# Clearing the sorted edge rows: blind from tile 1000 on, elsewhere only the padding, with the tile tables built inside the scatter

## What is computed

```python
h = relu(layernorm(x))
x = x + L0(h, edge_attr_64, ...)      # per edge: leaky_relu([h[dst], edge_attr] @ w1 + b1) @ w2 + b2, summed by src
x = x + L1(relu(layernorm(x)), ...)   # graph attention with 100 relation weights
x = x + L2(relu(layernorm(x)), ...)   # GCN: normalised sum over neighbours, mish
x = x + L3(relu(layernorm(x)), ...)   # mean over neighbours, relu
```

## Time and profile before

| | us |
|---|---|
| median of three runs | 3377.89 |
| the profiled execution, and its span | 3380.8, 3379.1 |
| block 1 | 0 to 180.8 |
| block 2: until the first indirect transfer | 181 to 280.2 |
| block 2: indirect transfers | 280.2 to 1310.5 |
| block 3 and the layers behind | 1318 to 3379.1 |

### The profile page before, as it was taken

One profiled execution on the slowest core, in us unless ns is written; L12 is line 12 of the kernel. 1 busy time (PEld: TensorE's weight loads), 2 busy tenths in 40 slices (PEclk: granted clock), 3 DMA queues, 4 the chain that ended last, 5 costly groups with the idle time before them and its releaser, 6 DMA issues. The chain is left out here.

```text
span 3379.1 us, 87741 instructions
## 1 busy us (share of the span) xinstructions
PE 2511.1 (74%) x20390; PEld 1974.6 (58%) x20391; DVE 2597.0 (77%) x8325; ACT 1489.4 (44%) x3942; POOL 1952.3 (58%) x2344
## 2 busy tenths in 40 slices
PE   1433555555555554999999999999999239989899
PEld 1322334333334343999999999999997214445455
DVE  7863777777777773999999999999997779983501
ACT  2011222222222222677777777777775655452200
POOL 1005777777777777899999999999996000000000
PEclk9975677677777776999999999999999559999999
DMA  9993222222222223888888888888886669869766
GB/s 381 414 414 129 78 78 83 78 78 78 77 79 78 78 68 104 236 240 234 242 239 235 240 239 234 242 238 236 241 239 226 255 282 343 301 219 315 249 220 208
DMA packets 738172, 696.84 MB, mean 206 GB/s; under 512 B 48524, under 2 KB 637275, under 8 KB 734779
## 3 DMA queue, kind: packets, MB, share of 16 engines
q1 hardware_dynamic: 516770, 536.77, 47.6%
q10 hardware_dynamic: 195544, 104.71, 12.7%
q0 software_dynamic: 25792, 54.52, 4.9%
HBM read 340.91 MB, written 354.90 MB: 206 GB/s over the span
## 5 line engine op out<-in xcount | busy, mean ns | idle before, releaser
L855 POOL DMA_INDIRECT sorted_rows<-rows,posi x806 | 785.1, 974 | 338.7 <-issue 221.4
L1147 DVE SCALAR_TENSOR_TENSOR acc<-acc,keep,pm 128x256 f32<-128x256 f32 x1504 | 715.7, 476 | 70.9 <-issue 23.9
L965 POOL TENSOR_SCALAR ohs_e<-iota,rt 128x128 f32<-128x128 f32 x1128 | 666.2, 607 | 12.4 <-DMA rt<-sorted_rows 12.4
L803 PE MATMUL s_peq<-sb_w1bb,eT 128*128 128x256 f32 x806 | 352.5, 531 | 398.9 <-ACT eT L658 379.9
L1074 PE MATMUL pm<-ohw_e,ohs_e 128*128 128x128 f32 x3008 | 609.1, 283 | 0.0
L974 POOL TENSOR_TENSOR hid<-pre_e,excess 128x512 f32<-128x512 f32 x376 | 482.8, 1284 | 117.2 <-ACT excess L1001 117.2
L1080 PE MATMUL px<-PN,dT 128*128 x4512 | 498.1, 219 | 0.4 <-ACT dT L1014 0.4
L1020 ACT ACTIVATE ohw_e<-ohd_e,rt 128x128 f32<-128x128 bf16 x1504 | 490.5, 397 | 0.0
L1074 PEld LDWEIGHTS pm<-ohw_e,ohs_e 128*128 128x128 f32 x3008 | 461.8, 194 | 0.0
L803 PEld LDWEIGHTS s_peq<-sb_w1bb,eT 128*128 128x128 f32 x806 | 172.8, 265 | 441.1 <-ACT eT L658 432.7
L1091 PE MATMUL ps<-hid,ohs_e 128*128 128x129 f32 x3008 | 424.3, 283 | 0.5 <-POOL hid L974 0.5
(11 more groups left out here) (317 smaller groups left out, 4206.3 us busy)
## 6 DMA issues: line engine op xcount, KB each, us to landing
count_matrices<-acc SPq DMA_DIRECT2D x1504, 128.0 KB, 2.6
sorted_rows<-zrow SPq DMA_DIRECT2D x188, 528.0 KB, 10.5
rt<-sorted_rows ACTq DMA_DIRECT2D x184, 528.0 KB, 4.6
gab<-count_matrices SPq DMA_DIRECT2D x60, 1280.0 KB, 6.0
arb<-count_matrices SPq DMA_DIRECT2D x25, 1664.0 KB, 8.8
ab<-count_matrices SPq DMA_DIRECT2D x25, 1600.0 KB, 9.3
arb<-count_matrices SPq DMA_DIRECT2D x25, 1536.0 KB, 8.5
ef<-in_edge_attr_dram SPq DMA_DIRECT2D x58, 364.0 KB
```

The source lines that it names most:

```text
L803: nc.tensor.matmul(pe_q[:, q % 2, 0:2 * D], eT[:, q % 2, :], w1bb[:], start=True, stop=True).then_inc(s_q, 1)
L855: pool.indirect_dma_start(sortd, bass.IndirectOffsetOnAxis(ap=posi[:, h, c:c + 1], axis=0), rows[:, h, c, :], None).then_inc(s_sc[h], 16)
L965: last = nc.gpsimd.tensor_scalar(ohs[:, k % BUFS, j, :], iota128[:], rt[:, k, j, D + 1:D + 2], None, ALU.is_equal)
L1147: nc.vector.scalar_tensor_tensor(acc[:, k % SUMS, j, :], before, keep[:, at:at + 1] if isinstance(at, int) else keep[:, ds(at, 1)], pm[:, ...
```

## The change

- **Clearing.** SP clears only tiles 1000 to 1503 blindly: 63 transfers of 8 tiles, all in block 1. Of tiles below 1000 only padding is cleared, rounded up to a multiple of 16 rows: for each bin the last 64, the 64 before them, the 32 or the 16 rows in front, as the bits of its padding say. The indices are computed on DVE, stored to device memory, loaded back with five bins in each of 125 partitions, and used by 20 indirect transfers on POOL (four sizes, five columns each; a row of such a transfer has 33,792, 16,896 or 8,448 bytes). Two more clear the tiles that round up a source tile's last bin to groups of four, and four more the free tiles below 1000. An index beyond tile 1000 writes nothing. POOL issues these 26 at the end of block 1.
- **One-hots** are made 52 columns at a time, with 16-bit inputs and outputs that are all contiguous along the columns.
- **Order of block 1.** All one-hots come first; the layer norm, the scans, and the counts' arithmetic follow; the transposes of H stand apart from the counting, and the projections of the nodes come last. ACT takes over half of the copies of PN and HT and all of the small weights.
- **Tile tables.** The 36 + 12 passes move into block 2, between places (0,1) and begin (1,0) on DVE; no transposes are needed, since the table's layout is another. They are stored by ACT before the last chunk and loaded within it.
- Several buffers share memory (`tmem`, `S`, `H`, `keep`), and POOL clears 26 columns instead of two whole buffers at the start of block 2.

The diff, cut to its core:

```diff
-                CLEARED = TT // ZR * 7 // 10
+PADS = ((192, 64, 1), (128, 64, 2), (32, 32, 0), (16, 16, 0))
+EDGE = 1000
+            BLIND = EDGE // ZR
...
 block 1, SP:
                     sp.wait_ge(s_z, 2)
-                    with sp.Fori(0, CLEARED) as n:
-                        sp.dma_start(zv[ds(n, 1)].squeeze(0), zrow[:].rearrange("p k w -> p (k w)")).then_inc(s_zd, 16)
+                    with sp.Fori(BLIND, TT // ZR) as n:
+                        sp.dma_start(zv[ds(n, 1)].squeeze(0), zrow[:, 0:ZR, :].rearrange("p k w -> p (k w)")).then_inc(s_zd, 16)
...
 block 1, ACT:
                     act.wait_ge(s_dv, 3)
-                    act.dma_start(rowinc.rearrange("(a b) -> a b", a=NT), cnt[:, 6, :]).then_inc(s_bo, 16)
-                    act.wait_ge(s_bo, 16)
+                    act.dma_start(rowinc.rearrange("(a b) -> a b", a=NT), cnt[:, 6, :]).then_inc(s_st, 16)
+                    act.wait_ge(s_dv, 4)
+                    act.dma_start(padr.rearrange("k (s d) -> s k d", s=NT), pout[:]).then_inc(s_st, 16)
+                    act.dma_start(fullr, fout[:]).then_inc(s_st, 16)
+                    act.wait_ge(s_st, 48)
+                    with nc.allow_non_contiguous_dma(reason="five bins in each partition"):
+                        act.dma_start(padi[:], padr.rearrange("k (p c) -> p k c", p=PADP)).then_inc(s_pi, 16)
+                        act.dma_start(fulli[:], fullr.rearrange("s (j c) -> (s j) c", c=2)).then_inc(s_pi, 16)
                     act.dma_start(incb[:], rowinc.partition_broadcast(P)).then_inc(s_bo, 16)
...
 block 1, POOL:
+                    def clear(index, parts, size):
+                        spots = sortd.rearrange("(n s) w -> n (s w)", s=size)
+                        pool.indirect_dma_start(
+                            spots, bass.IndirectOffsetOnAxis(ap=index, axis=0),
+                            zrow[0:parts, 0:size, :].rearrange("p k w -> p (k w)"), None,
+                            bounds_check=EDGE * P // size - 1, oob_is_err=False).then_inc(s_cl, 16)
+                    pool.wait_ge(s_z, 6)
+                    pool.wait_ge(s_pi, 32)
+                    for k, (bits, size, back_) in enumerate(PADS):
+                        for c in range(BINS // PADP):
+                            clear(padi[:, k, c:c + 1], PADP, size)
+                    for c in range(2):
+                        clear(fulli[:, c:c + 1], 3 * NT, P // 2)
+                    pool.wait_ge(s_dv, 5)
+                    for c in range(4):
+                        clear(freei[:, c:c + 1], FREE, P // 2)
...
 block 1, DVE (one-hots):
-                        nc.vector.tensor_tensor(ohs[:, n % 2, 0:w, :], iota32[:].unsqueeze(1).to_broadcast([P, w, QP]),
-                                                tile[:, 1, c].unsqueeze(2).to_broadcast([P, w, QP]), ALU.is_equal)
+                        nc.vector.tensor_tensor(ohs[:, n % 2, :, 0:w], rep32[:, :, 0:w],
+                                                tile[:, 1, c].unsqueeze(1).to_broadcast([P, QP, w]), ALU.is_equal)
...
 block 2, SP:
-                    with sp.Fori(CLEARED, TT // ZR) as n:
-                        sp.dma_start(zv[ds(n, 1)].squeeze(0), zrow[:].rearrange("p k w -> p (k w)")).then_inc(s_zd, 16)
 block 2, DVE:
                     positions(0, 0, True)
                     places(0, 1)
+                    tables()
                     begin(1, 0, False)
                     positions(0, 1, True)
 block 2, ACT, around the last chunk:
+                    act.wait_ge(s_ts, 1)
+                    act.dma_start(tilef.rearrange("(p j) -> p j", j=TCOL), tilk[:]).then_inc(s_to, 16)
+                    act.dma_start(tiler.rearrange("k (p j) -> p k j", j=TCOL), tili[:, 0:3, :]).then_inc(s_to, 16)
                     step(BODIES - 1, False, True)
+                    act.wait_ge(s_to, 32)
...
+                    act.dma_start(keep[:], tilef[0:TT].partition_broadcast(P)).then_inc(s_tl, 16)
 block 2, POOL:
-                    nc.gpsimd.memset(ef[:], 0.0).then_inc(s_pad, 1)
-                    nc.gpsimd.memset(rows[:], 0.0).then_inc(s_pad, 1)
-                    pool.wait_ge(s_zd, 16 * (TT // ZR))
+                    nc.gpsimd.memset(rows[:, :, :, D + 3:D + 4], 0.0).then_inc(s_pad, 1)
+                    pool.wait_ge(s_zd, 16 * (TT // ZR - BLIND))
+                    pool.wait_ge(s_cl, 16 * (len(PADS) * (BINS // PADP) + 6))
```

More of the change, by code:

```diff
@@ L113, in build @@
         brow = {}
-        for name in ("b1", "bs", "bn"):
+        for name in ("bs", "bn"):
             brow[name] = tsb("row_" + name, [1, D])
@@ L276, in _ @@
-                    act.wait_ge(s_to, 32)
+                        if t % 4 == 3 and t >= 7:
+                            turned(t // 4 - 1)
+                    for g in range(NT // 4 - 1, NQ):
+                        turned(g)
+                    act.wait_ge(s_dv, 3)
+                    act.dma_start(rowinc.rearrange("(a b) -> a b", a=NT), cnt[:, 6, :]).then_inc(s_st, 16)
+                    act.wait_ge(s_dv, 4)
+                    act.dma_start(padr.rearrange("k (s d) -> s k d", s=NT), pout[:]).then_inc(s_st, 16)
@@ new lines, in _ @@
+                    for g in range(NQ + 1):
+                        if g < NQ:
+                            first(g)
+                        if g >= 1:
+                            second(g - 1)
+                    act.wait_ge(s_w, 1)
+                    for k, name in enumerate(("WsT", "WnT")):
+                        nc.scalar.activation(wl[name][:], px[:, 1, (2 + k) * P:(3 + k) * P], ACT.Copy)
+                    nc.scalar.activation(wturn[:].rearrange("p a b -> p (a b)"), px[:, 1, 0:2 * P], ACT.Copy).then_inc(s_wc, 1)
@@ L301, in _ @@
                     line(iota128[:], [[1, P]])
-                    nc.gpsimd.memset(later[:], 1.0).then_inc(s_pc, 1)
-                    pool.wait_ge(s_pc, 2)
+                    for k, (bits, size, back_) in enumerate(PADS):
+                        nc.gpsimd.memset(pmask[:, k:k + 1], bits)
+                        if not back_:
+                            nc.gpsimd.memset(pmask[:, k + 2:k + 3], -size)
+                    nc.gpsimd.memset(later[:], 1.0).then_inc(s_z, 1)
+                    pool.wait_ge(s_z, 4)
@@ new lines, in _ @@
+                    link(last)
+                    for k, (bits, size, back_) in enumerate(PADS):
+                        if not back_:
+                            last = nc.vector.scalar_tensor_tensor(pidx[:, 0, k, :], cnt[:, 0, :], float(P // 2 // size), part[:, k - 2, :],
+                                                                  ALU.mult, ALU.subtract)
+                    link(last)
+                    nc.vector.tensor_tensor(pout[:], pidx[:, 0, :, :], pidx[:, 1, :, :], ALU.add)
@@ L455, in _, with turn @@
+                    nc.vector.tensor_copy(lo[:], raw[:, 0:2, :])
+                    nc.vector.tensor_copy(typ[:], raw[:, 2, :])
+                    for g in range(NQ + 1):
+                        if g < NQ:
+                            rest(g)
+                        if g >= 1:
+                            third(g - 1)
+                    nc.vector.tensor_tensor(X[:], X[:], c2bc[:].unsqueeze(1).to_broadcast([P, NT, D]), ALU.add)
                 @block.tensor
                 def _(pe):
+                    def turn(g):
+                        if g >= 2:
+                            pe.wait_ge(s_ln["copied"], g - 1)
+                        pe.wait_ge(s_ln["h"], min(4 * g + 4, NT))
+                        for t in range(4 * g, min(4 * g + 4, NT)):
+                            last = nc.tensor.transpose(tp[:, g % 2, (t % 4) * P:(t % 4 + 1) * P], H[:, t, :], ident[:])
+                        last.then_inc(s_ln["turned"], 1)
@@ L463, in project @@
                             nc.tensor.matmul(px[:, g % 2, o:o + D], HT[:, t * P:(t + 1) * P], wl["w1a"][:], start=True, stop=False)
-                            last = nc.tensor.matmul(px[:, g % 2, o:o + D], ones[0:1, :], brow["b1"][:], start=False, stop=True)
+                            last = nc.tensor.matmul(px[:, g % 2, o:o + D], ones[0:1, :], b1bc[0:1, :], start=False, stop=True)
                         last.then_inc(s_pn, 1)
-                    pe.wait_ge(s_con, 3)
+                    pe.wait_ge(s_con, 1)
                     for n in range(NS):
```

387 lines of the change are left out of this document (222 added, 165 removed).

## The result

The changed kernel takes 3476.6 us (median of four runs, 3462.4 to 3482.2) against 3376.7 for the kernel before in the same session: a ratio of 1.0289, 95% interval 1.0256 to 1.0322. It is **slower by 100 us**, where 85 us of gain were forecast. The profiled execution took 3482.2 us, its span is 3480.4.

A forecast was written before the change was run, and what follows sets the result against it. Clearing was taken to hold the scatter's start, POOL's calls to pace the rest. Block 2 at 138 plus 73.5 us to second positions puts call 14 at 211.5, 85 us earlier: 3380.8 becomes 3295, median 3293; range 3278 to 3330.

The forecast's parts named there:

- Where the change is decided: Start of POOL's scatter call 14: moves from 296.9 to 211.5, 85 us earlier; later calls and blocks go on as they are.
- Clears and counts: Block 1: SP's 63 clears issued until 89 us, one-hot counting done at 53, POOL's clearing calls starting at 104.
- rival 2: One-hot compares in block 1 stay at the old speed: counting ends 24 us later, call 14 at 236, 3317 us; chance 0.07.
- The price of a call: POOL's 26 indirect clearing calls in block 1 take 1.28 us each, until 137.
- rival 3: POOL's clearing calls cost by their bytes: POOL leaves block 1 at 294, call 14 at 368, 3448 us; chance 0.07.
- Landing: Padding's 26.7 MB land in 65 us at 414 GB/s, 83 with 12.4 of 16 engines; landed at 189 us.
- Rival 1: Padding lands late: five engines a call, 95 us, call 14 at 218, 3299 us; one engine, 126 us, 3330; chance 0.2.
- Start of block 2: POOL, PE with ACT, and DVE finish block 1 at 134 to 137, so block 2 starts at 138 instead of 181.
- The tables: DVE's tables in block 2 take 33.2 us, second positions ready 73.5 us in; padding's landing covers all but 5 us.
- Rival 4: No gain: the scatter's start is not bound by clearing and call 14 stays; chance 0.02.

The follow-up runs named there:

- e3: The changed kernel with 128 index rows instead of 125 in the twenty padding calls, the three added out of range: 3362.2 us, 0.994 to 0.997 of the kernel before.
- e1: The changed kernel with the 26 indirect clearing calls moved from the end of POOL's block 1 to the head of its block 2: 3437.7 us.
- e12: e8 with the ten calls of 32 and 16 rows and the four free ones moved to the head of POOL's block 2: 3310.3 us.
- e8: The changed kernel with 128 index rows in all 26 calls, bins dealt one by one to partitions, tables at the end of DVE's block 1: 3315.0 us.
- e2: The changed kernel with the tile tables computed at the end of DVE's block 1 instead of inside the scatter: 3434.2 us.
- e5: The changed kernel with 128 index rows in the twenty padding calls and the tile tables at the end of DVE's block 1: 3330.6 us.

## Why the prediction was wrong, step by step

- **Where the change is decided: right.** Call 14 moved by 103.1 us, the span by 101.3; the pace behind it is unchanged (1.276 us a call), and so is what follows: 2069.9 us from call 806 to the end, 2069.6 before.
- **Clears and counts: nearly right.** The 63 clears were issued by 90.7 (89 forecast). Compares of 1664 elements took 1.02 us (1.0), so rival 2 falls:

```profile
21.80 1.02 DVE L420 TENSOR_TENSOR S<-keep,tile 128x1664 f16<-128x1664 f16 x1
...
36.10 1.03 DVE L420 TENSOR_TENSOR S<-keep,tile 128x1664 f16<-128x1664 f16 x1 [6.46 <-PE hist L572]
```

  The counting still ended at 61 instead of 53: the fifth step began at 36.1 (33 forecast), and three later waits of DVE for PE, 5.6 us in all, were not in the sum. POOL's first call came at 109.4 (104 forecast, although 91 and two times 5 make 101).
- **The price of a call: 1.28 forecast, 1.49 measured** at 125 rows and 1.27 at 128. It does not go by bytes, so rival 3, the only one that made the kernel slower, falls: the time did rise, but by another road. The 26 calls took 40 us instead of 33, under the landing.
- **Landing: the first step that failed.** "At 414 GB/s ... 65 us", at most 83, "because nothing suggests that the load is spread anew". Measured 218 us. The step took a rate from direct transfers of 128 partitions and corrected it only for idle engines, in blocks of eight partitions that no row shows. What the runs showed in its place: an indirect call's landing goes by how its rows are cut (102 us with 128 rows, same bytes, e3). Rival 1 named the right cut, a call of 125 rows on five engines, and its sign, a first scatter call behind 200, came (351.5). But it priced the call by the bytes of the busiest engine at full speed: 95 us. The busy engines ran at half that speed (175 GB/s at 0.84), and the load was more uneven than it reckoned: over the last 78 us the share was a quarter or less on average.
- **Start of block 2: the second.** "POOL leaves block 1 at 137 ... All three agree, so block 2 starts at 138". This took a transfer to be over for its engine once issued. For SP that holds. SP's queue in the kernel before, its last clears of block 1 (start, time until the last was issued):

```profile
159.16 21.19 SPq L232 DMA_DIRECT2D sorted_rows<-zrow  x16
```

  They were issued until 180.35, block 2 began at 181.0, and a clear takes 10.5 us to land, so block 2 did not wait for the last of them to land. For POOL's indirect transfers it does not hold (e1, and e12 against e8): the block's end waited for all of them.
- **The tables: right in size, wrong in cover.** 73.5 us from the start of block 2 to call 14 were forecast, 72.3 measured. The cover was to be the landing; but since the barrier stands behind the landing, none of it was left, and the 32 us came on top (e2).
- **Rival 4 falls too:** clearing held the start of the scatter as before, only for longer.

Together: block 2 at 327.7 instead of 138 is 190 us. With the landing as forecast (83 + 2 us from 109.4) block 2 would have begun near 194, since it waits for that: some 56 us of the 190 are the barrier and a first call 5 us late, some 133 the landing. Without the barrier the same landing would have cost less, since call 14 of e1 is 27 us earlier although its calls start 34 us later. With 128 rows (e3) the change is a gain of 0.5%, with the tables ahead of the barrier as well (e5) of 1.4%.

## What to carry to other kernels

A transfer's price is its shape: the same 26.7 MB landed in 84 to 329 us, depending on how many index rows a call had and on which partitions they stood (the 329 include POOL's stops at 127 rows); here it paid to fill a call up to 128 rows, be it with rows that write nothing, and to deal the valid ones over all partitions. Ask of each engine whether a block's end waits for its transfers to be issued or to land, and put long ones of the latter kind where something else still runs. Work that was hidden beneath a wait must be placed again when the wait moves.

## What the runs showed of the hardware that was not expected

- Among the clearing calls a call's time on POOL goes with its packets and not with its bytes: 0.90 us with 80 packets (64 rows), 0.96 with 144, 1.18 with 416, 2.5 to 3.0 with 2048 (127 rows), and then POOL stops for up to 158 us between calls. Packets are not all of it: the scatter's calls have 32 and take 0.96 too.
- Rows out of range cost almost nothing in the transfer: 8320 empty packets lengthened the landing by 5 us.
- An indirect transfer from 128 partitions reaches what direct clearing does, 407 GB/s at a full share in e3:

```profile
115.00:140.00 25.00, 23.23 (x66) 16.02 (x67) 7.88 (x12) 6.29 (x14) 19.21 (x20) 1.00 1.00 407
```
